# Causal self attention: keys after the query cleared by GpSimd instead of a TensorE product, maxima in order of width; stacks of both self attentions in 4 KB pieces

## The reference, cut to what matters

```python
# layer 0: causal
att = jnp.einsum('bhqd,bhkd->bhqk', q, k) / jnp.sqrt(jnp.float32(D))
att = jnp.where(causal[None, None], att, -jnp.inf)
att = jax.nn.softmax(att, axis=-1)
y = jnp.einsum('bhqk,bhkd->bhqd', att, v)
# layer 1: every key, q and k normed per head
q = _rmsnorm(q, q_norm_w)
k = _rmsnorm(k, k_norm_w)
attn = jax.nn.softmax(jnp.einsum('bnhd,bmhd->bhnm', q * scale, k), axis=-1)
```

## Time and profile before

| | us |
|---|---|
| median of 3 runs | 2481.39 |
| lowest, highest | 2476.70, 2486.93 |
| profiled execution, own time | 2478.18 |
| its span | 2476.3 |

### The profile page before, as it was taken

The page is one execution under the profiler, slowest core; times in us unless marked ns, Lnnn a source line. Parts: engine busy times, 40 slices in busy tenths (PEclk is TensorE's granted clock), DMA queues, the critical chain, the costliest instruction groups (busy, mean ns, idle before and its releaser), DMA issues. The chain is left out here.

```text
span 2476.3 us, 44303 instructions
## 1 busy us (share of the span) xinstructions
PE 2249.2 (91%) x13992; PEld 1427.4 (58%) x13993; DVE 1413.6 (57%) x3651; ACT 1188.7 (48%) x2803; POOL 743.6 (30%) x848
## 2 busy tenths in 40 slices
PE   7999999878996799899999999889985899999998
PEld 5444554344655567643333333345553799999997
DVE  4676666435874444577777777366654543434343
ACT  1666666623442463267777776533322433333332
POOL 3111111033531321233322321055430533333333
PEclk9999999989998899999999999999998999999999
DMA  6344444214221310323333333110009221222221
GB/s 162 104 131 124 130 125 125 65 39 136 83 78 43 102 53 1 90 76 103 106 94 105 99 100 99 41 33 10 10 3 375 66 38 32 38 33 37 35 36 23
DMA packets 160823, 197.00 MB, mean 80 GB/s; under 512 B 27238, under 2 KB 121104, under 8 KB 160528
## 3 DMA queue, kind: packets, MB, share of 16 engines
q1 hardware_dynamic: 145008, 175.47, 22.8%
q0 software_dynamic: 13680, 17.84, 4.5%
q10 hardware_dynamic: 1968, 1.60, 0.5%
HBM read 124.83 MB, written 70.12 MB: 79 GB/s over the span
## 5 line engine op out<-in xcount | busy, mean ns | idle before, releaser
L485 ACT ACTIVATE self_probs<-self_score_ps 128x512 f32<-128x512 f32 (+3 forms) x1024 | 479.6, 516 | 261.9 <-PE self_score_ps L856 151.9
L653 DVE TENSOR_REDUCE self_neg_max<-self_max_ps 128x1 f32<-128x512 f32 x512 | 328.6, 685 | 125.8 <-PE self_max_ps L842 122.2
L842 PE MATMUL self_max_ps<-self_k_stack,self_q_stack 96*128 96x512 bf16 (+3 forms) x1024 | 348.9, 343 | 32.9 <-DVE self_neg_max L650 21.8
L853 PE MATMUL self_score_ps<-self_q_stack,self_k_stack 99*128 99x512 bf16 (+3 forms) x1024 | 346.0, 345 | 13.4 <-ACT self_probs L485 13.2
L2758 ACT ACTIVATE x_stream<-experts_up_ps,experts_bias_now 128x128 f32<-128x128 f32 x568 | 161.9, 368 | 351.7 <-PE experts_up_ps L2970 351.7
L650 DVE CUSTOM_DVE_ANT_0 self_masked<-self_max_ps,self_later 128x128 f32<-128x128 f32 (+3 forms) x512 | 234.8, 488 | 128.0 <-PE self_max_ps L842 120.4
L2970 PEld LDWEIGHTS experts_up_ps<-experts_tileT,x_stream 128*128 128x128 f32 x2272 | 267.4, 194 | 5.2 <-issue 1.7
L2970 PE MATMUL experts_up_ps<-experts_tileT,x_stream 128*128 128x128 f32 x2272 | 267.8, 277 | 1.3 <-DVE x_stream L2880 1.3
L2980 PE MATMUL experts_down_ps<-experts_down,x_stream 128*128 x1136 | 256.8, 379 | 0.0
L853 PEld LDWEIGHTS self_score_ps<-self_q_stack,self_k_stack 99*128 99x128 bf16 x1024 | 99.3, 98 | 248.4 <-ACT self_probs L485 181.0
L867 PE MATMUL self_out_ps<-self_probs,self_values 128*32 128x512 f32 (+3 forms) x2048 | 235.1, 531 | 6.7 <-ACT self_o_raw L471 4.8
(11 more groups left out here) (339 smaller groups left out, 3783.9 us busy)
## 6 DMA issues: line engine op xcount, KB each, us to landing
self_parts_dram<-self_parts SPq DMA_DIRECT2D x64, 384.0 KB, 2.7
self_q_stack<-self_parts_dram SPq DMA_DIRECT2D x384, 64.0 KB, 2.3
self_k_stack<-self_parts_dram SPq DMA_DIRECT2D x360, 64.0 KB, 2.3
self_out_dram<-self_o_raw SPq DMA_DIRECT2D x60, 256.0 KB, 2.1
crossx_out_dram<-crossx_o_raw SPq DMA_DIRECT2D x16, 512.0 KB, 2.7
experts_up<-moe_up_dram SPq DMA_DIRECT2D x8, 1024.0 KB, 8.7
experts_down<-moe_down_dram SPq DMA_DIRECT2D x8, 1024.0 KB, 10.7
self_o_now<-self_out_dram SPq DMA_DIRECT2D x30, 256.0 KB
```

Of the source, the lines that this page charges most:

```text
L485: act.activation(probs[:, i % 8, 0:w], score_ps[:, (16 * n + i) % 3, 0:w], ACT.Exp).then_inc(exp_done, 1)
L653: dve.tensor_reduce(neg_max[:, n % 2, t, h:h + 1], max_ps[:, i % 2, 0:w], AX, ALU.max, negate=True).then_inc(max_read, 1)
L842: last = pe.matmul(max_ps[:, i % 2, 0:w], q_stack[0:ROWS, h, P * t:P * t + P], k_stack[0:ROWS, h, 0:w], start=True, stop=True)
L853: last = pe.matmul(score_ps[:, m % 3, 0:w], k_stack[0:KROWS, head, P * j:P * j + P], q_stack[0:KROWS, head, S - w:S], start=True, stop=not ...
```

## The change

- The causal product L856 is gone. POOL's `clear_later` sets the later keys of the diagonal square of a step's four exponentials to zero, an affine select over 4 x 128 elements of each partition, and `with_values` waits for it. `probs` becomes three steps deep in the causal stage, and in step 0 `with_values` of the step before stands behind the fourth score tile instead of the second.
- POOL's queue in the causal stage is written anew: `cut_shift(n + 2)` ahead of the clear of step 3, the third parts and `inverse_deviation` between clears.
- Causal maxima go by width: 4 tiles of 512, then 384, 256, 128.
- The 128 rows of an item are ordered by feature, then head, by another order of the weights' columns on the host. So four heads of a feature lie together in the scratch, now [item, part, row, token], and a stack is moved in 3 transfers for queries and 3 for keys of 192, 128 and 64 KB in 4 KB pieces, for keys from one part repeated 3, 2 and 1 times. The store of an item is in 1 KB pieces instead of 3 KB. SP's and ACT's stacks both use this.
- `sum_squares` multiplies by `same_head` instead of `head_ones`; DVE makes it by two operations at the start of the second stage.

```diff
@@ -128,7 +130,7 @@
-        probs = sb("probs", [P, 8, S])
+        probs = sb("probs", [P, PROBS * GH, S])
@@ -147,7 +149,9 @@
-        scratch = nc.dram_tensor(f"{name}_parts_dram", [4, P, 3, S], BF16).ap()
+            one_head = sb("one_head", [P, 8])
+            same_head = sb("same_head", [P, P])
+        scratch = nc.dram_tensor(f"{name}_parts_dram", [4, 3, P, S], BF16).ap()
@@ -183,6 +188,9 @@
+        def maximum_of(i):
+            return (i % GH, TT - 1 - i // GH) if causal else (i // TT, i % TT)
@@ -233,6 +241,18 @@
+        def stack_rows(half, g, which):
+
+            stk, item = (q_stack, k_stack)[which], 2 * half + which
+            heads = slice(GH * (g % 2), GH * (g % 2) + GH)
+            for r, count in ((0, 3), (3, 2), (5, 1)):
+                dst = stk[HD * r:HD * (r + count), GH * g:GH * g + GH, :].rearrange("r h t -> r (h t)")
+                if which == 0:
+                    yield dst, scratch[item, 0:count].rearrange("c (d h) t -> (c d) h t", h=8)[:, heads]
+                else:
+                    one = scratch[item, 3 - count].rearrange("(d h) t -> d h t", h=8)[:, heads].rearrange("d h t -> d (h t)")
+                    yield dst, one.unsqueeze(0).to_broadcast([count, HD, GH * S])
@@ -257,21 +277,18 @@
-                        wait(sp, stacked[2 * half], 192 * b)
-                        wait(sp, stacked[2 * half + 1], 192 * b)
-                        sp.dma_start(scratch[item], parts[:, item]).then_inc(parts_stored[half], 16)
+                        wait(sp, stacked[2 * half], 96 * b)
+                        wait(sp, stacked[2 * half + 1], 96 * b)
+                        sp.dma_start(scratch[item].rearrange("c p t -> p c t"), parts[:, item]).then_inc(parts_stored[half], 16)
...
-                        for r, part in enumerate(which):
-                            sp.dma_start(stk[HD * r:HD * r + HD, GH * g:GH * g + GH, :],
-                                         scratch[item, rows, part, :].rearrange("(h d) t -> d h t", d=HD)
-                                         ).then_inc(stacked[g], 16)
+                    for which in range(2 if both else 1):
+                        for dst, src in stack_rows(half, g, which):
+                            sp.dma_start(dst, src).then_inc(stacked[g], 16)
@@ -354,6 +371,13 @@
+                def clear_later(n, j):
+                    u = 4 * n + j
+                    pool.wait_ge(exp_done, 4 * u + 4)
+                    square_now = probs[:, GH * (u % PROBS):GH * (u % PROBS) + GH, 0:P]
+                    pool.affine_select(out=square_now, in_=square_now, compare_op=ALU.is_ge, fill=0.0, base=0,
+                                       pattern=[[0, GH], [1, P]], channel_multiplier=-1).then_inc(later_cleared, 1)
@@ -391,34 +415,47 @@
+                if causal:
+                    cut_shift(1)
+                    for n in range(N):
+                        b, g = n // NG, n % NG
+                        for j in range(TT):
+                            if j == TT - 1 and n + 2 < N:
+                                cut_shift(n + 2)
+                            clear_later(n, j)
+                            if b + 1 < B and g < 2 and j in (1, 2):
+                                third_part(b + 1, 2 * g + j - 1)
+                            if b + 2 < B and (g, j) == (1, 0):
+                                inverse_deviation(b + 2)
@@ -723,6 +759,11 @@
+                if norm:
+                    dve.tensor_reduce(one_head[:], c.ident[:].rearrange("p (d h) -> p h d", h=8), AX, ALU.max).then_inc(same_head_made, 1)
+                    dve.wait_ge(same_head_made, 1)
+                    dve.tensor_copy(same_head[:].rearrange("p (d h) -> p d h", h=8),
+                                    one_head[:].unsqueeze(1).to_broadcast([P, HD, 8])).then_inc(same_head_made, 1)
@@ -851,20 +893,21 @@
-                                     q_stack[0:KROWS, head, S - w:S], start=True, stop=not causal)
-                    if causal:
-                        last = pe.matmul(score_ps[:, m % 3, 0:P], c.ident_b[:], c.causal_kq[:], start=False, stop=True)
+                                     q_stack[0:KROWS, head, S - w:S], start=True, stop=True)
...
-                    pe.wait_ge(exp_done, 16 * n + 4 * j + 4)
+                    if causal:
+                        pe.wait_ge(later_cleared, 4 * n + j + 1)
+                    else:
+                        pe.wait_ge(exp_done, 16 * n + 4 * j + 4)
@@ -896,7 +939,7 @@
-                            if h == 1 and (n, j) != (0, 0):
+                            if h == (3 if causal and j == 0 else 1) and (n, j) != (0, 0):
@@ -3041,9 +3084,9 @@
-        "l0_qk": np.ascontiguousarray(qkv0[:, :2 * D]), "l0_v": np.ascontiguousarray(qkv0[:, 2 * D:]),
+        "l0_qk": np.ascontiguousarray(qkv0[:, mod_order[:2 * D]]), "l0_v": np.ascontiguousarray(qkv0[:, 2 * D:]),
```

More of the change, by code:

```diff
@@ L105, in sem @@
         return s
+    PROBS = 3 if causal else 2
     with ExitStack() as ctx:
@@ L393, in _ @@
                     square(1, 1)
[L394 to L421, removed]
@@ new lines, in _ @@
+                if causal:
[11 more added lines that the diff above has]
+                else:
+                    for b in range(B):
+                        cut_shift(4 * b + 1)
+                        if b + 1 < B:
+                            if norm:
+                                scale_rows(b + 1, 0)
+                                scale_rows(b + 1, 1)
+                            third_part(b + 1, 0)
+                            if norm:
+                                square(b + 1, 2)
+                            third_part(b + 1, 1)
+                            if norm:
+                                square(b + 1, 3)
+                        cut_shift(4 * b + 2)
+                        if b + 1 < B:
+                            if norm:
+                                scale_rows(b + 1, 2)
+                                scale_rows(b + 1, 3)
+                            if b + 2 < B:
+                                inverse_deviation(b + 2)
+                            third_part(b + 1, 2)
+                            third_part(b + 1, 3)
+                            add_bias(b + 1)
+                        cut_shift(4 * b + 3)
+                        if b + 1 < B:
+                            cut_shift(4 * b + 4)
+                        if norm and b + 2 < B:
+                            square(b + 2, 0)
+                            square(b + 2, 1)
@@ L483, in exponentials @@
                     if h == 0:
-                        wait(act, pv_done, 4 * n + j - 1)
-                    act.activation(probs[:, i % 8, 0:w], score_ps[:, (16 * n + i) % 3, 0:w], ACT.Exp).then_inc(exp_done, 1)
+                        wait(act, pv_done, 4 * n + j - PROBS + 1)
+                    act.activation(probs[:, GH * ((4 * n + j) % PROBS) + h, 0:w], score_ps[:, (16 * n + i) % 3, 0:w], ACT.Exp).then_inc(exp_done, 1)
                 def between(b, g, j, half):
@@ L543, in stack_keys @@
                     act.wait_ge(parts_stored[0], 32)
-                    for r, part in enumerate(K_PART):
-                        act.dma_start(k_stack[HD * r:HD * r + HD, GH * g:GH * g + GH, :],
-                                      scratch[1, 64 * g:64 * g + 64, part, :].rearrange("(h d) t -> d h t", d=HD)).then_inc(stacked[g], 16)
+                    for dst, src in stack_rows(0, g, 1):
+                        act.dma_start(dst, src).then_inc(stacked[g], 16)
                 transposed(0, 0)
@@ L642, in maximum @@
                 def maximum(n, i):
-                    h, t = i // TT, i % TT
+                    h, t = maximum_of(i)
                     if i == 0:
@@ L783, in sum_squares @@
                     pe.wait_ge(sq_done, 4 * b + i + 1)
-                    pe.matmul(general[:, bank("s", b, i)], c.head_ones[:], squares[:, i % 2], start=True, stop=True).then_inc(ss_full, 1)
+                    pe.wait_ge(same_head_made, 2)
+                    pe.matmul(general[:, bank("s", b, i)], same_head[:], squares[:, i % 2], start=True, stop=True).then_inc(ss_full, 1)
                 def value_rows(b, t):
@@ L866, in with_values @@
                     for h in range(GH):
-                        last = pe.matmul(out_ps[32 * h:32 * h + 32, S - w:S], values[:, b % 2, j, GH * g + h], probs[:, (4 * j + h) % 8, 0:w],
+                        last = pe.matmul(out_ps[32 * h:32 * h + 32, S - w:S], values[:, b % 2, j, GH * g + h], probs[:, GH * ((4 * n + j) % PROBS) + h, 0:w],
                                          start=(j == 0), stop=(j == TT - 1), tile_position=(0, 32 * h))
```

17 lines of the change are left out of this document (9 added, 8 removed).

## The result

The changed kernel takes 2512.1 us (median of 4 runs, 2509.4 to 2514.4) against 2479.9 us (2476.7 to 2486.9) for the kernel before, measured beside it: a ratio of 1.0125, 95% interval 1.0104 to 1.0145. It is slower by 1.25%, some 31 us. The forecast was 2474 us with a range up to 2500, so both the time and its sign were missed. The profiled execution took 2509.4 us, its span 2507.6.

What follows compares the result with a forecast made beforehand. TensorE was taken as nearest to the limit in the causal loop, its idle mostly DVE lagging. Terms -16 - 0.5 + 2 + 7 = -7.5 us took 2481.4 to 2474 us, range 2456 to 2500.

Steps and rivals of the forecast that it cites:

- The product, the order, the clear: Causal loop: removed product and maxima by width, less the clear, save 2.4 us a batch over 6.7 batches, -16 us.
- The clear: GpSimd's affine select in the causal stage: taken at 0.7 us each, bounds 0.52 and 1.35 us.
- Rival 2: Causal loop: a clear of 1.35 us becomes the wait, kernel slower at 2499 us; chance 0.12.
- The tail: Last two causal groups, without maxima: three or four clears lie open, some 0.7 us each, less causal products, +2 us.
- The stacks: Causal loop: a batch's first key stack and shift row land 1.0 us late in 7 batches, +7 us.
- The clock: Causal loop: forecast wrong if idle of near 1 us before step 0 lowers the clock; no price given.
- Rival 3: Causal loop and second stage: stacks take 12.6 us to landing, 3.0 us late x 7, 2492 us; chance 0.13.
- The other three stacks: Causal loop: a batch's stacks other than the first have 2.5 us or more to spare.
- The opening: Start of the causal stage: first key stack 1 us later (-1 to +3), maxima by width give about 1 us; 0.
- The second stage: Second self attention: fillers and other waits cover the opening, the same stack has 1.4 us spare; 0.
- What would show it: Signs listed: batch period 52.9 to 54.3 us, TensorE waiting about 1 us every third group, DMA share 0.19 then 0.12.

Runs made afterwards that it cites:

- e1: Changed kernel with the repeats of each key stack moved one by one, on 16 engines instead of 3, 2 and 1: 2468.3 us.
- e4: As e1, with both third parts of a half issued by GpSimd behind the clear of step 1: 2470.3 us.
- e8: As e1, with the key stacks of the depths stage moved repeat by repeat too: 2458.0 us.
- e13: As e1, with each 64 KB source written as 2 blocks of 8 rows: 2465.5 us.
- e10: Kernel before with the 512 causal products left out and nothing in their place: 2467.5 us.
- e7: As e1, with the maxima in the order of the kernel before, head by head: 2478.0 us.
- e11: As e1, with the clears left out: 2461.4 us.
- e6: As e1, with each clear done twice, one behind the other: 2502.4 us.
- e9: Changed kernel with repeats moved one by one in the second, third and fourth stack of a batch, not the first: 2491.9 us.
- e5: Changed kernel with repeats moved one by one in the first stack of a batch alone: 2494.4 us.
- e2: Kernel before with only the new stacks and stores, and the depth and head order they need: 2514.8 us.
- e14: As e13, but the two blocks come from two parts so they can't be joined: 2550.5 us.

## Why the prediction was wrong, point by point

- *The product, the order, the clear: -16 in the loop.* Right in sum. e1 runs from its first to its 31st group in 390.8 us, the kernel before in 405.4: 14.6 less, with a batch of 53.7 (53.3 forecast). The profiled execution of e1 took 2480.3 us, 12 above its median, but not because of this loop: e4, e8 and e13 run it in 390.7 too. The parts were mis-sized against each other: the product is worth 2.0 us a batch and not 2.5 (e10), and the order mostly hides the clear (e7 against e10 and e11).
- *The clear: 0.7 us.* Measured 0.635. The bounds from the memset and the 128 wide select held it, near the lower one. Rival 2's price for a clear of 1.35 us was close too: 2499 less 2467 (the forecast without the stacks' 7) is 32 us, and e6 is 34 above e1, with 3.2 us a batch in the loop (4.3 reckoned) and more in the last groups.
- *The tail: +2.* From the start of the 31st group to the cross attention's first maximum the kernel before takes 53.3 us, the changed kernel 55.3 and e1 56.4: +2 and +3. Kernels with the same causal code scatter here up to 60.5 (e8), so this term is not known to better than some us.
- *The stacks: +7, bounds 0 and +21.* This is the step that failed. Measured on the changed kernel against e1, group by group, the loop is 40.9 us longer. It splits into three: in six batches the group that ends in the wait for the shift rows is 3.3 to 5.2 us longer, 24.0 us in sum (23.0 of it the wait itself), where 1.0 each was taken; 14 us in the step or two behind them (1.4 to 2.9 us longer than in e1 each time); and 2.7 us of ScalarE waiting for the sums in the first batch.
  - The landing was nearly right: 10.8 us (10.6 from the depths stage and the shift rows behind it) taken, 11.3 in the batch shown and 12.0 on the mean of the six: 1.2 of the 3 us by which each batch is later than forecast.
  - The start was wrong, and it is the other 2: 3.6 us into the group taken, 5.6 measured on the mean (5.5 in the batch shown). The same stack starts at 2.8 to 4.1 in e1, and at 3.2 to 4.4 in e9, where the first stack is as in the changed kernel and the others are quick; the moved third parts and the store in 1 KB pieces are in both, so neither explains it. In e5, where the first stack is quick and the others are slow, it starts at 3.7 to 6.1. What the prediction did not follow is what the other stacks do to the transfers behind them. The way it goes is read from SP's queue and not tried by itself. SP waits for the output store behind the fourth stack to land before it issues the outputs' loads, 0.9 to 1.9 us in each of the six batches (0.2 us at most in the kernel before, nothing in e1), and the first of the two stores of the parts is queued behind those. The second store is not late: its third part on GpSimd releases it 0.54 us before the group starts, in e1 and in the changed kernel alike. So loads and both stores now travel together, and the second lands later. e1's queue (its group starts at 234.33), then the changed kernel's (253.98); the second store is issued at the end of the row of stores:

```profile
229.70 0.63 SPq L314 DMA_DIRECT2D self_o_now<-self_out_dram  x1
231.09 3.08 SPq L283 DMA_DIRECT2D self_parts_dram<-self_parts  x2
237.93 1.25 SPq L292 DMA_DIRECT2D self_q_stack<-self_parts_dram  x3
```

```profile
250.24 0.64 SPq L313 DMA_DIRECT2D self_o_now<-self_out_dram  x1
251.65 2.16 SPq L282 DMA_DIRECT2D self_parts_dram<-self_parts  x2
```

  - The clock was named as something that would make it wrong and given no price. At 0.50 it costs 14 us, more than half as much as the waits themselves. Of the 19 such waits in the changed kernel, e2 and e9, the clock fell to 0.50 at or around the group's start in 13, and these groups are 1.4 to 3.2 us longer; in the other six it stayed at 1.00, and they are 0.01 us longer. Whether it falls doesn't follow from the wait's length alone: in e2 a wait of 3.19 us left the next step at its usual 4.36 us, and one of 3.52 made it 7.31.
- *Rival 3* had the mechanism, and nearly the size of the wait: 3.0 us a batch, 21 in all, where 4.0 and 24 came. In part that is luck: it had all of its lateness from a slower landing (12.6 us, 12.0 measured) and none from the start. Its time, 2492, lacked the clock, the opening and the output chain. It had 0.13. The rule of the Trainium skill (DMA: Bandwidth & Descriptors, Why a DMA increments its semaphore by 16 and not by 1) that stood beside it agrees with the runs here: outermost 3 gave a share of 0.18, outermost 2 (e14) 0.12 to 0.14, 16 (e1) 0.63 to 1.00. With e13, written with an outermost 2 and moved at 0.99, it agrees only if the two blocks were joined.
- *"The other three stacks have 2.5 us or more."* They have for their own waiters. Their cost is for others: e5, with the first stack repaired, still loses 26 us to e1 through the output store.
- *The opening: 0, bounds -1 and +3.* +2.1: the loop starts at 64.97 (62.88 before, 62.74 in e1). The first maximum waits till 43.20, against 40.89 in the earlier trace rows.
- *The second stage: 0.* Right: the first six batches of the second self attention take 401.4 us after and 401.0 before. (Single executions scatter there: e13 took 402.1 and e1 407.4, half of what e1's profiled execution lies above its median.)
- *What would show it.* The list named the right rows: waits at the start of every third group, DMA share 0.19 and 0.12, a loop whose clock falls. The reading was sound; the sum gave the small value to a term whose bounds went three times further, and those bounds themselves assumed that this stack alone was slow.

In one line: -14.6 in the loop and +2 to +3 behind it for the clear and its order, then +24.0 +14 +2.7 +2.1 for the stacks: 30 to 31 us, against 30.4 at the cross attention's first maximum.

## What to carry to other kernels

Here a transfer ran on as many engines as its outermost size, 3, 2 or 16. So write repeats as separate transfers even where that means more of them: nine transfers on 16 engines had all landed 5.8 us after the first issue (e1: 237.93, last issue 241.53, 2.2 to its landing) where six, three of them on 3, 2 and 1, held the shift rows behind them till 11 us or more. When a transfer gets slower, follow not only its own waiter but every transfer issued behind it, and what the issuing engine waits for among those, once around the loop. And where a term's upper bound would leave TensorE standing for some us in each round, add the price of the lower clock behind it.

## What the runs showed of the hardware

- An affine select in place over 4 x 128 float32 elements of 128 partitions took 0.635 us on GpSimd; two in a row took 0.638 each (the second began 0.70 after the first).
- From the first issue of a stack whose key side (384 KB) ran on 3, 2 and 1 engines to the landing of the shift rows behind it 11.1 to 13.4 us went by, on two engines 13.1 us (the one shown); on 16 engines a 64 KB transfer of it landed 2.8 us after its issue (median).
- A source view split in two contiguous blocks moved at a share of 0.99, like one of 16 rows (e13); two blocks from different places moved at 0.12 to 0.14 (e14).
- Two engines moved 49 GB/s, with a source that a transfer repeats (changed kernel) and without (e14).
- Granted 0.50 for some 3 us after a standstill of 3.11 us cost 1.4 us in one group's first step; the largest such cost in the changed kernel's loop was 2.9.
